# Two layers' per-sample matrices: one layer's built before the first convolution in one half of PSUM, the other's in pairs behind four stages

## What is computed

```python
x = x + conv(x, L0_weight, groups=4, 9 taps, padding 4) + (cond @ L0_c_weight.T)[:, :, None] + fside[None, :, None]
x = x + expert(x, cond, L1_...)
x = x + conv(x, L2_weight, ...) + ...        # as the first
x = x + expert(x, cond, L3_...)              # as the second

def expert(x, cond, W0, b0, W1, b1, W2, b2, weight, bias_k):
    h = gelu(gelu(cond @ W0 + b0) @ W1 + b1)
    att = softmax(h @ W2 + b2)                       # (128 samples, 8 experts)
    agg_w = einsum('bk,koi->boi', att, weight)       # a 128 x 128 matrix of each sample
    return einsum('boi,bih->boh', agg_w, x) + (att @ bias_k)[:, :, None]
```

## Time and profile before

| | us |
|---|---|
| median of 3 runs (2658.6 to 2659.79) | 2659.2 |
| the profiled execution | 2658.37 |
| its span, first to last instruction | 2656.6 |
| mean granted TensorE clock | 0.984 |
| TensorE busy | 2588.4 (97%) |
| VectorE busy | 2148.2 (81%) |
| ScalarE busy | 1493.2 (56%) |
| GpSimd busy | 36.7 (1%) |

### The profile page before, as it was taken

The page is one execution under the profiler, slowest core; times in us unless marked ns, Lnnn a source line. Parts: engine busy times, 40 slices in busy tenths (PEclk is TensorE's granted clock), DMA queues, the critical chain, the costliest instruction groups (busy, mean ns, idle before and its releaser), DMA issues.

```text
span 2656.6 us, 57542 instructions
## 1 busy us (share of the span) xinstructions
PE 2588.4 (97%) x24812; PEld 1191.4 (45%) x24812; DVE 2148.2 (81%) x815; ACT 1493.2 (56%) x852; POOL 36.7 (1%) x31
## 2 busy tenths in 40 slices
PE   6689999999999999999999999999999999999998
PEld 4234444444444444444444444444444444444443
DVE  5678888888888888888888888888888888888883
ACT  2345555555555555555555555555555555555554
POOL 5000000000000000000000000000000000000000
PEclk8689999999999999999999999999999999999999
DMA  4543444434434434444344344343443443443433
GB/s 151 205 163 118 155 121 130 146 118 136 140 118 146 130 119 152 123 127 149 118 139 137 118 150 126 120 154 120 132 144 118 139 137 118 148 128 120 153 92 112
DMA packets 185493, 357.06 MB, mean 134 GB/s; under 512 B 12714, under 2 KB 143794, under 8 KB 152634
## 3 DMA queue, kind: packets, MB, share of 16 engines
q1 hardware_dynamic: 184576, 352.37, 42.3%
q10 hardware_dynamic: 898, 4.39, 0.7%
HBM read 205.72 MB, written 150.99 MB: 134 GB/s over the span
## 4 chain that ended last, share of the span: by engine, by line
PE 96%; DMA 2%; DVE 1%; ACT 1%; issue 0%; ACTq 0%; SPq 0%; DVEq 0%
PE psum L350 34%; PE psum L313 33%; PE psum L325 28%; DMA mix_dram<-y 1%; DVE diff L545 0%; DVE y L594 0%; ACT y L464 0%; DMA select_sb<-select 0%; PE psum L274 0%; ACT y L474 0%; PE psum L303 0%; DMA mixw<-mix_dram 0%; ACT x L514 0%; ACT outb L498 0%; DVE att L565 0%
## 5 line engine op out<-in xcount | busy, mean ns | idle before, releaser
L545 DVE TENSOR_TENSOR diff<-xin 128x2052 f32<-128x2052 f32 x256 | 986.7, 3897 | 354.9 <-PE psum L325 354.9
L350 PE MATMUL psum<-y,mixw 32*128 32x512 f32 x8192 | 917.8, 595 | 20.1 <-DMA mixw<-mix_dram 13.7
L313 PE MATMUL psum<-diff,prod_w 32*128 32x512 f32 x8192 | 907.8, 589 | 12.5 <-DVE bias_table L584 7.6
L325 PE MATMUL psum<-diff,prod_w 32*128 32x512 f32 (+1 forms) x8192 | 773.2, 600 | 0.0
L471 ACT COPY shared<-psum 128x2048 f32<-128x2048 f32 x256 | 477.8, 1866 | 381.7 <-PE psum L313 375.4
L350 PEld LDWEIGHTS psum<-y,mixw 32*128 32x128 f32 x8192 | 418.5, 186 | 503.6 <-issue 497.9
L313 PEld LDWEIGHTS psum<-diff,prod_w 32*128 32x128 f32 x8192 | 430.4, 186 | 466.9 <-issue 458.9
L474 ACT COPY y<-psum 128x2048 f32<-128x2048 f32 x256 | 478.1, 1867 | 272.8 <-PE psum L325 272.8
L545 DVE TENSOR_TENSOR diff<-x 128x2055 f32<-128x2055 f32 x256 | 571.1, 2295 | 10.3 <-ACT x L514 10.3
L325 PEld LDWEIGHTS psum<-diff,prod_w 32*128 32x128 f32 (+1 forms) x8192 | 315.8, 158 | 434.2 <-issue 417.4
L514 ACT ACTIVATE x<-psum,bias_now 128x2048 f32<-128x2048 f32 x128 | 252.7, 1974 | 215.8 <-PE psum L350 215.8
(11 more groups left out here) (57 smaller groups left out, 92.4 us busy)
## 6 DMA issues: line engine op xcount, KB each, us to landing
xin<-x SPq DMA_DIRECT2D x128, 1024.0 KB, 6.6
out<-outb SPq DMA_DIRECT2D x128, 1024.0 KB, 4.7
mixw<-mix_dram SPq DMA_DIRECT2D x512, 128.0 KB, 5.2
mix_dram<-y SPq DMA_DIRECT2D x16, 1024.0 KB, 4.4
y<-experts ACTq DMA_DIRECT2D x2, 512.0 KB, 12.4
x<-conv_w ACTq DMA_DIRECT2D x1, 768.0 KB, 9.5
shared<-conv_w ACTq DMA_DIRECT2D x1, 768.0 KB, 10.9
diff<-expert_rows ACTq DMA_DIRECT2D x4, 144.0 KB
```

Of the source, the lines that this page charges most:

```text
L313: mm = pe.matmul(psum[:, half, g, :], prod_w[v][at, kind, s, :], diff[at, s, :, 0:R], start=first and s == 0, stop=last and s == PH - 1, s ...
L325: return pe.matmul(psum[cols, half, g, :], prod_w[v][at, kind, s, cols], diff[at, s, :, 0:R], start=False, stop=stop, skip_group_check=True)
L350: mm = pe.matmul(psum[:, half, r, :], mixw[m][at, b, g, :], y[m][at, :, g, b, :], start=g == 0, stop=g == GROUPS - 1)
L545: nc.vector.tensor_tensor(into(kind), in0, in1, op).then_inc(diff_ready[v], 1)
```

## The change

Layer 0's eight sets move ahead of front(0), into the setup. They all go through half A; ScalarE makes all eight copies, and set j+1 waits for the copy of set j (`first_taken`). Behind sets 0 and 2 TensorE does spread(0) and spread(1), behind 4 and 6 fold_bias(0) and fold_bias(1), both in half B. front(0) starts behind the last copy.

Layer 1's eight sets go in four pairs, one set in each half: behind front(0), behind first_mix(0), behind front(1) and behind middle(1) (`two_more`). ScalarE copies the set of half A, VectorE that of half B (`stage_next`, counted by `next_taken`); the last pair is staged in shared[0] (`late_staging`). The sync engine's stores and the loads of x(1), x(2) and the mix weights are ordered to match, and x(0) is loaded only when wide has landed.

The setup waits for wide alone and later for the small loads by semaphores of their own; expert rows 0, select and experts are issued ahead of the taps. A one-element Gelu is issued ahead of the wait for wide. VectorE makes x(0)'s BOTH and SIGNED first and the other two behind the second scaling of beta; for pair 1 it puts set 3's copy between the two couples. The loop body has the same instructions and waits as before.

```diff
         staging = y[1][:].rearrange("p j g b r -> p j (g b r)").rearrange("p j (r c) -> p j r c", r=PH)
+        late_staging = shared[0][:]
...
                 for b in range(PB):
                     sp.dma_start(xin[:, b * XROW + PH:b * XROW + PH + L], x[PB * n + b]).then_inc(x_loaded, 16)
 
-            def store_agg(m):
+            def store_agg(m, j, source):
+                sp.dma_start(mix_dram[m].rearrange("b (r c) -> b r c", r=PH)[:, :, j * BANK:(j + 1) * BANK],
...
-                    q = m * SETS + j
-                    if q % 2 == 0:
-                        sp.wait_ge(agg_act, q // 2 + 1)
-                    else:
-                        sp.wait_ge(agg_dve, q // 2 + 1)
-                    sp.dma_start(mix_dram[m].rearrange("b (r c) -> b r c", r=PH)[:, :, j * BANK:(j + 1) * BANK],
-                                 staging[:, q % 2]).then_inc(agg_stored[q % 2], 16)
+                    sp.wait_ge(first_taken, j + 1)
+                    store_agg(0, j, staging[:, j % 2])
+
+            def store_next(sets, source):
+                for j in sets:
+                    sp.wait_ge(next_taken[j % 2], j // 2 + 1)
+                    store_agg(1, j, source[:, j % 2])
+
+            def all_stored(m):
...
             sp.wait_ge(diff_ready[0], PRODUCTS)
             load_x(1)
+            all_stored(0)
+            load_mix(0, 0)
 
             def step(i):
                 if whole(i) and i == 0:
-                    store_agg(0)
-                    load_mix(0, 0)
+                    store_next((0, 1), staging)
+                    sp.wait_ge(mix_done[0], PB)
+                    load_mix(0, 1)
+                    store_next((2, 3), staging)
                 if whole(i) and i == 1:
...
+                    all_stored(1)
                     load_mix(1, 0)
...
@@ -204,7 +221,7 @@
                 if not (whole(i) and i + 2 >= PAIRS):
...
                 e = pool.memset(xin[:, b * XROW + PH + L:(b + 1) * XROW], 0.0)
             e.then_inc(edges_clear, 1)
...
-            pe.wait_ge(par_loaded, PAR_LOADS)
+            pe.wait_ge(par_loaded, 16)
...
+            pe.wait_ge(small_loaded, SMALL_LOADS)
...
                 pe.wait_ge(mlp_act, 3 + m)
                 pe.matmul(psum[:, m, 2, 0:EXPERTS], hid[m]["h1"][:], par[m]["w2"], start=True, stop=False)
@@ -268,42 +286,47 @@
                     mm = pe.matmul(psum[CG * r:CG * r + EXPERTS, m, 3, 0:B], hid[m]["att"][:], eye_sb,
                                    start=True, stop=True)
                 mm.then_inc(mlp_pe, 1)
-            for m in range(2):
-                pe.wait_ge(att_t_ready, 1 + m)
+            def spread(m):
+
+                if m == 0:
+                    pe.wait_ge(select_loaded, 16)
+                else:
+                    pe.wait_ge(scaled_ready, 1)
                 for k in range(EXPERTS):
-                    mm = pe.matmul(psum[:, m, k // 4, B * (k % 4):B * (k % 4 + 1)], select_sb[:, k, :],
+                    mm = pe.matmul(psum[:, B_HALF, k // 4, B * (k % 4):B * (k % 4 + 1)], select_sb[:, k, :],
                                    hid[m]["att_t"][0:EXPERTS, :], start=True, stop=True)
                 mm.then_inc(spread_pe, 1)
...
 
+                if m == 0:
+                    pe.wait_ge(experts_loaded, 32)
                 pe.wait_ge(scaled_ready, m + 1)
-                pe.wait_ge(experts_loaded, 32)
-                into = psum[:, m, 2, 0:B]
+                into = psum[:, B_HALF, 2 + m, 0:B]
...
-            for m in range(2):
-                fold_bias(m)
...
+            def aggregate(m, j, half):
+
+                for r in range(PH):
+                    mm = pe.matmul(psum[:, half, r, :], hid[m]["att_t"][CG * r:CG * r + EXPERTS + 1, :],
+                                   rows[m][CG * r:CG * r + EXPERTS + 1, j * BANK:(j + 1) * BANK],
+                                   start=True, stop=True)
+                mm.then_inc(agg_pe, 1)
+
+            pe.wait_ge(att_t_ready, 2)
+            pe.wait_ge(rows_loaded[0], 16 * PH)
+            for j in range(SETS):
+                if j >= 1:
+                    pe.wait_ge(first_taken, j)
+                aggregate(0, j, A)
+                if j in (0, 2):
+                    spread(j // 2)
+                if j in (4, 6):
+                    fold_bias((j - 4) // 2)
...
             def front(i):
                 if whole(i) and i == 0:
-                    pe.wait_ge(bias_ready, 2)
+                    pe.wait_ge(first_taken, SETS)
+                elif whole(i) and i == 1:
+                    pe.wait_ge(next_taken[0], 2)
                 else:
                     pe.wait_ge(x2_ready, PB * (i - 1) + 1)
-                pe.wait_ge(diff_ready[0], PRODUCTS * i + 3)
+                pe.wait_ge(diff_ready[0], PRODUCTS * i + (1 if whole(i) and i < 2 else 3))
                 pe.wait_ge(taps_ready, 1)
                 product(0, BOTH, A, True, False)
-                if not (whole(i) and i == 0):
+                if whole(i) and i == 0:
+                    pe.wait_ge(bias_ready, 2)
+                elif whole(i) and i == 1:
+                    pe.wait_ge(next_taken[1], 2)
+                else:
                     pe.wait_ge(x2_ready, PB * (i - 1) + 2)
-                pe.wait_ge(diff_ready[0], PRODUCTS * i + 4)
+                pe.wait_ge(diff_ready[0], PRODUCTS * i + (2 if whole(i) and i < 2 else 4))
                 product(0, SIGNED, B_HALF, True, False)
+                if whole(i) and i < 2:
+                    pe.wait_ge(diff_ready[0], PRODUCTS * i + 4)
                 outer_products(0, i)
 
...
                 if has_back(i):
                     pe.wait_ge(out_ready, PB * (i - 2) + 1)
                 else:
-                    pe.wait_ge(sums_taken[0], 2 * i + 1)
+                    pe.wait_ge(next_taken[0], 3)
...
                 if has_back(i):
                     pe.wait_ge(out_ready, PB * (i - 2) + 2)
                 else:
-                    pe.wait_ge(sums_taken[0], 2 * i + 2)
+                    pe.wait_ge(next_taken[1], 3)
...
             def first_mix(i):
-                if whole(i) and i == 0:
-                    pe.wait_ge(agg_act, SETS // 2)
-                    pe.wait_ge(agg_dve, SETS // 2)
+                if whole(i) and i < 2:
+                    pe.wait_ge(next_taken[0], 3 * i + 1)
                 else:
                     pe.wait_ge(sums_taken[1], 2 * (i - 1) + 1)
                 pe.wait_ge(y_ready[0], 2 * i + 2)
                 pe.wait_ge(mix_loaded[0], MIX_LOADS * (i + 1))
                 mix(0, A, 0)
-                if not (whole(i) and i == 0):
+                if whole(i) and i < 2:
+                    pe.wait_ge(next_taken[1], 3 * i + 1)
+                else:
                     pe.wait_ge(sums_taken[1], 2 * (i - 1) + 2)
                 mix(0, B_HALF, 1)
+
+            def two_more(j, released, count):
+
+                if j == 0:
+                    pe.wait_ge(rows_loaded[1], 16 * PH)
+                pe.wait_ge(released, count + 1)
+                aggregate(1, j, A)
+                pe.wait_ge(released, count + 2)
+                aggregate(1, j + 1, B_HALF)
 
...
-                if whole(i) and i <= 1:
-                    pe.wait_ge(sums_taken[0], 2 * i + 2)
-                    aggregate(i)
-                if whole(i) and i == 1:
-                    pe.wait_ge(agg_act, SETS)
-                    pe.wait_ge(agg_dve, SETS)
+                if whole(i) and i < 2:
+                    two_more(4 * i, sums_taken[0], 2 * i)
                 if has_back(i):
                     last(i)
                 if has_middle(i):
                     middle(i)
+                if whole(i) and i == 1:
+                    two_more(6, sums_taken[1], 0)
                 if has_front(i):
                     first_mix(i)
+                if whole(i) and i == 0:
+                    two_more(2, x2_ready, 0)
 
...
             act.dma_start(wide_sb[:], wide).then_inc(par_loaded, 16)
-            act.dma_start(bias_k_sb[:], bias_k).then_inc(par_loaded, 16)
-            act.dma_start(b2_sb[:], b2).then_inc(par_loaded, 16)
-            act.dma_start(select_sb[:], select).then_inc(par_loaded, 16)
+            act.dma_start(b2_sb[:], b2).then_inc(small_loaded, 16)
+            act.dma_start(bias_k_sb[:], bias_k).then_inc(small_loaded, 16)
+            for r in range(PH):
+                act.dma_start(rows[0][CG * r:CG * r + EXPERTS + 1, :],
+                              expert_rows[0][:, r * SLICE:(r + 1) * SLICE]).then_inc(rows_loaded[0], 16)
+            act.dma_start(select_sb[:], select).then_inc(select_loaded, 16)
+            for m in range(2):
+                act.dma_start(expert_sb[m], experts[m]).then_inc(experts_loaded, 16)
             for v in range(2):
                 act.dma_start(taps[v], conv_w[v]).then_inc(taps_loaded, 16)
...
+            for r in range(PH):
+                act.dma_start(rows[1][CG * r:CG * r + EXPERTS + 1, :],
```

(67 more changed lines are left out.)

55 lines of the change are left out of this document (14 added, 41 removed).

## The result

The changed kernel takes 2639.39 us (median of 4, 2638.4 to 2640.52) against 2659.4 (median of 4, 2658.6 to 2659.79): ratio 0.9925 [0.9913, 0.9938]. The forecast was 2630, its range 2617 to 2641: the gain is 20 where 29 was forecast. The profiled execution took 2638.4, its span is 2636.6, 20.0 less than before.

A forecast was written before the change was run, and what follows sets the result against it. TensorE's work bounds the loop; ahead of it, the old set blocks are bound by copy and store latency in turn. 17.5 + 38 + 14.9 + 33 + 35 = 138.4 against 167.3, 28.9 less: 2630 us, range 2617 to 2641.

The forecast's parts named there:

- The bound, the loop and the end: Whole kernel: TensorE's work alone sets the loop; the gain comes ahead of it and the other 2489 us stay.
- M: End of first_mix(1), from which TensorE's work is unbroken; 167.3 us before, forecast 138.4.
- Part 1: Setup chain up to set 0: starts 2.5 us earlier, last attention copy ends at 17.5, bounds 17.0 and 20.0.
- Part 2: Layer 0's eight sets ahead of front(0): 38 us at mostly low clock, bounds 27 and 40.
- the ring no longer binds: Layer 0's sets: 4.0 us for set and copy exceeds 3.2 for the store ring over two buffers.
- Late rows: Setup rival: 9-partition expert-row loads are slow; rows[0] in at 25 instead of before 17.5, 7.5 later, 2638; chance 0.12.
- Part 3: front(0): takes 14.9 us, so its end F is 70.4, 14.6 later than before.
- Part 4: F, the end of front(0), to F1, the end of front(1): 33 us with a cold mix, F1 at 103.4.
- Part 5: End of front(1) to M: 35 us, between 33.2 if warm throughout and 39.0 if middle and mix start cold.
- warm setup: Eight-set setup rival: the clock rises early, 27 us instead of 38, M about 123, kernel 2615; chance 0.13.
- Cold stages: Rival for front(0)'s end to M: waits keep the clock low, 112 us, M at 182, kernel 2674; chance 0.03.
- no gain: Rival for front(0)'s end to M: stages do not hide layer 1's sets, 95 us, kernel 2657; chance 0.02.

The follow-up runs named there:

- experiment 5: One-element early Gelu left out, once in the changed kernel (2641.53 us, ratio 0.9935), once in experiment 4 (2630.19 us, ratio 0.9889).
- experiment 3: Changed kernel with layer 0's sets 2 and 3 staged in shared[0], so no copy before set 4's waits for a store: 2635.08 us, ratio 0.9905.
- experiment 4: Changed kernel with half of rows[0]'s columns and all rows[1] loads issued behind stores, fewer issues on ScalarE: 2627.9 us, ratio 0.9887.
- Experiment 2: Changed kernel with rows[1] behind the eighth copy, and four same-size loads over 128 partitions in their old place: 2635.72 us, ratio 0.9911.
- experiment 7: Changed kernel with x(0) loaded at once instead of behind the wide load: 2640.87 us, ratio 0.9932.
- 6: Changed kernel with select, experts, taps and rows[1] issued by the sync engine behind x(0) instead of by ScalarE: 2642.4 us, ratio 0.9934.
- 1: Changed kernel with the four rows[1] loads moved behind the last copy of a set: 2632.53 us, ratio 0.9904.
- 8: Changed kernel without layer 1's eight sets, copies and stores (layer 3 takes layer 0's matrices, different result): 2614.49 us, ratio 0.9831.

## Why the prediction was right or wrong, step by step

**The bound, the loop and the end: right.** The whole change lies ahead of M, to 0.8 us. Those 0.8 are the last mix (10.22 against 9.42), which was 8.58 to 10.22 in the kernels run here and follows a wait of over 4 us in each; a term that I had left out and that scatters. The next-to-last mix, 7.15 in both traces, is 8.85 in five others, so that it cancels in this pair is luck.

**Part 1, the setup chain: the time right (17.3 for 17.5), one assumption idle.** I took "wide in by 8.5" as the condition. It was in at 4.2 and never bound; ScalarE's issues did, to 8.2 (7.6 forecast), as the step had it. The first Gelu stood at 9.63, 0.4 later than forecast, and from it to set 0 it took 7.7 where I had carried over 8.3: two small errors that cancel. The early Gelu, which the step put on the path as 0.3, hides nothing there (experiment 5). Its table load takes 1.28, and the next ACTIVATE starts 1.30 after the load's start (8.22, 9.52). By that, this trace does not agree with the 2.66 us that the Trainium skill, page "ScalarE: Activation LUTs", section "What ACT_TABLE_LOAD costs", books for a switch. Nor does the later change from Gelu to Exp, whose load starts at 11.67 and whose ACTIVATE at 12.96. Experiment 5 measured 1.27 for having it early (6.50 - 5.23).

**Part 2, the eight sets: the step that failed.** From set 0 to front(0) it took 45.1, not 38. The sets, copies and pieces between were right: set 1 starts 4.9 after set 0 (forecast 5.3), set 4 to set 5 is 6.2 (6.6), set 3 to set 4 is 4.1 (4.0). Without the wait, priced at 6.6 by experiment 3, it is 38.5, and experiment 4 has 38.5. The sentence that failed is "the ring no longer binds". It set 4.0 a set against (1.87 + 4.5)/2 = 3.2 and took the 4.5 from the earlier trace rows, the median of stores in blocks where little else moved (eight of 1 MB in the 38 us of the earlier trace rows make some 220 of its 235 GB/s, by my estimate). In the setup the store shared the engines with the loads onto 9 partitions and with 4.5 MB of x(0), experts and taps: 14.87. Experiment 2 splits the excess of 10.5: some 6 for the form of rows[1], which is shown, and some 4 that I put down to the bulk. With 14.87 in its place the same formula gives 8.4 a set, so for store 0 the ring does bind. The mis-sized term is the store, 14.9 for 4.5, at a price of 6.6 us of path.

**Late rows, the third rival: the cause right, the victim wrong.** I had the rate of the nine-partition loads from the earlier trace rows and asked only whether rows[0] would come late to set 0. They did not (experiment 7 shows when they do); rows[1], four loads behind, came in the way of the store. The rival's time, 2638, is near what was measured, by another wait; that is luck. I priced a slow load by its own user and not by the others who use the engines while it runs.

**Part 3: right.** front(0) took 14.90 for 14.9.

**Part 4, F to F1: right.** F1 = 110.33, 33.0 after F. The wait for a difference stands in front(1) (2.24), the first mix is cold (9.65).

**Part 5, F1 to M: right, near its middle.** 36.2 for 35. The copy to shared waits for the store of set 5 (10.41), which lands 14.0 after F1 (14.6 forecast), and TensorE waits 2.80 for it (3). The outer products took 7.50 (5.86 warm) and the mix 8.85 (6.87 warm, 9.68 cold): each in part at the low level, between the ends that I gave.

**The sum.** 17.3 + 45.1 + 14.9 + 33.0 + 36.2 = 146.5 against 138.4. Of the 8.1, 7.1 are part 2, 6.6 of them the wait. In experiment 4, with the same sets and no store awaited, the terms after set 0 make 38.5 + 14.8 + 69.1 = 122.5 where the forecast had 120.9.

**The other rivals.** The warm setup did not come: sets 0, 2, 3 and 4 take 2.09 each, set 6 1.75, and the folds 3.78 for 16 instructions. Cold stages did not come either: front(1)'s first products take 7.16, against 6.87 warm. The rule cited there (the Trainium skill, page "TensorE: Matmul & The Clock Gate", section "A second HAM failure mode: psum-queue depth-cycling") is that small idle gaps between groups that cycle through PSUM make the clock fall and rise again. The trace agrees as far as it goes: between F and M the granted clock is 0.50 at 82 to 86 us, at 114 to 116, at 128 to 130 and at 139 to 141, and 1.00 from 88 to 110, from 118 to 124 and at 132 to 134. What did not come is the rival's step from there, that the low level stays from F to M. That rival was also mis-added: it took 0.9 for a warm set where the earlier trace rows give 1.32 (two in 2.64), and the trace has 1.04 to 1.61 for the sets between F and M. The sum of the forecast does not use it. And the fourth rival, no gain, had 95 from F to M, where 69.2 were measured.

**Left open.** From F to M it is 69.1 or 69.2 in the changed kernel and in experiments 4 and 6, but 71.5 to 72.9 in the other six traces that have all four pairs. This is not the price of an earlier front(0): experiment 4 starts it earliest, at 51.20, and is short, while experiment 7 starts it last, at 64.75, and has 72.5, and experiment 5's first kernel, at 62.38, has 71.5. The three short traces have the store of set 5 in 4.46 to 4.47, the six others in 5.42 to 6.32, and then 1.0 to 1.3 more in the outer products or in the mix behind it, at the lower clock. Why that store is slower there was not tried, and a difference in M of less than 4 us can't be put down to an edit for this reason. Two kernels' loops (3 and 6) are 2.3 longer from M to the next-to-last mix than all others (2451.55 for 2449.2 to 2449.3), with mixes of 7.10 where 7.06 stand elsewhere; this has no cause that I could find in the change of either. The next-to-last mix itself takes 7.15 before, after and in experiments 1, 4, 7 and 8, and 8.85 in 2, 3, 6 and both of 5, also without a cause that I know.

## What to carry to other kernels

A store's or load's time from a quiet stretch is not its time in a busy one: when work is moved into the setup, ask what else is in the DMA engines at that moment, and give every user of them, not the slow load's own alone, the later time. Loads onto few partitions went well here when issued in parts between the stores (experiment 4), and badly in a row ahead of them. Issuing is work of the issuing engine: on the engine that stands in the critical chain it delays the first instruction, and moved to another queue it puts small loads behind large ones.

## What the runs showed of the hardware

- Four loads of 144 KB onto 9 partitions delayed a 1 MB store from another queue by some 6 us more than the same bytes over 128 partitions: 14.87 us from issue to landing against 8.5, and 9.40 with neither. It landed at 36.2, 30.2 and 28.4.
- The granted-clock column was no guide here before its first fall. A window of the changed kernel (us, then busy us and count of TensorE, its weight loads, VectorE, ScalarE and GpSimd, the granted clock, DMA share, GB/s):

```profile
17.00:30.00 13.00, 10.67 (x48) 7.05 (x49) 7.35 (x11) 3.73 (x2) 3.05 (x2) 1.00 0.96 324
```

and one of experiment 4:

```profile
14.00:25.00 11.00, 8.99 (x42) 5.88 (x39) 6.73 (x10) 4.70 (x3) 4.21 (x2) 0.50 0.96 370
```

In both a set of eight takes 2.09, against 2.64 for sixteen at full clock, though one reads 1.00 and the other 0.50. Whether such an early stretch ran at 1.2 or 2.4 GHz is to be read from the durations of its matmuls.
